# Causal mask of the row maxima: added by a TensorE matmul with the identity, the maxima by VectorE's plain negated reduction

## The reference, cut to what matters

```
q = shape_heads((hidden_states @ wq.T + bq) * scaling)
k = shape_heads(hidden_states @ wk.T + bk)
scores = jnp.einsum('bhtd,bhsd->bhts', q, k)
mask = jnp.triu(jnp.full((T, T), -10000.0, dtype=jnp.float32), k=1)
attn = jax.nn.softmax(scores.astype(jnp.float32) + mask, axis=-1).astype(jnp.float16)
out = jnp.einsum('bhts,bhsd->bhtd', attn, v)
```

## Time and profile before

| | |
|---|---|
| device time, median of 3 | 1112.86 us (1111.68 to 1113.47) |
| span of the profiled execution | 1105.8 us |
| TensorE matmul busy | 838.2 us, 76% |
| VectorE busy | 718.5 us, 65% |
| ScalarE busy | 521.4 us, 47% |
| GpSimd busy | 429.1 us, 39% |
| mean granted TensorE clock | 0.688 of full speed |

### The profile page before, as it was taken

How to read it: one execution, slowest core, us unless ns; L and a number is a source line. 1 busy time by engine, 2 the same in 40 slices (tenths; PEclk the granted TensorE clock), 3 DMA queues, 4 the chain that set the end, 5 groups by cost and what they waited for, 6 DMA issues and landing times. The chain is left out here.

```text
span 1105.8 us, 24845 instructions
## 1 busy us (share of the span) xinstructions
PE 838.2 (76%) x6684; PEld 499.3 (45%) x6685; DVE 718.5 (65%) x2639; ACT 521.4 (47%) x982; POOL 429.1 (39%) x452
## 2 busy tenths in 40 slices
PE   3698977688769678776895219999999999999600
PEld 1133433233233233332332108778778877877500
DVE  4766786787878776877875535555555555555366
ACT  2266554546446455545465015454545445454234
POOL 2145454554636546545557531222112222111224
PEclk9555555555555555555555559999999999999855
DMA  4011010210111201101110023111111111111067
GB/s 142 1 46 52 27 56 27 65 61 29 46 52 40 59 27 45 54 26 57 54 43 27 29 79 101 44 43 38 34 43 43 43 43 43 33 39 44 30 212 244
DMA packets 52749, 61.27 MB, mean 55 GB/s; under 512 B 5264, under 2 KB 39696, under 8 KB 52688
## 3 DMA queue, kind: packets, MB, share of 16 engines
q1 hardware_dynamic: 46896, 46.14, 13.9%
q0 software_dynamic: 5792, 14.49, 3.7%
HBM read 37.71 MB, written 22.90 MB: 55 GB/s over the span
## 5 line engine op out<-in xcount | busy, mean ns | idle before, releaser
L550 ACT ACTIVATE pT<-bank 128x512 f16<-128x512 f32 (+1 forms) x384 | 194.8, 527 | 241.1 <-PE bank L906 240.1
L652 DVE CUSTOM_DVE_ANT_0 unused<-bank,mask 128x384 f16<-128x384 f32 (+3 forms) x512 | 233.5, 485 | 68.3 <-PE bank L897 51.0
L897 PE MATMUL bank<-kT,qT 32*128 32x384 f16 (+3 forms) x512 | 181.3, 454 | 67.4 <-DVE nmax L652 65.1
L1354 PE MATMUL bank<-xT,gu_part 128*128 128x256 f16 (+1 forms) x1716 | 201.3, 275 | 5.0 <-issue 4.0
L1202 POOL DMA_INDIRECT expert_rows<-y_sb,dest x78 | 74.8, 959 | 315.5 <-DVE y_sb L1314 303.6
L442 POOL TENSOR_SCALAR_AFFINE_SELECT pT<-pT 128x512 f16<-128x512 f16 x128 | 80.3, 639 | 269.6 <-ACT pT L550 268.9
L1354 PEld LDWEIGHTS bank<-xT,gu_part 128*128 (+1 forms) x1716 | 166.4, 100 | 40.1 <-issue 14.0
L906 PE MATMUL bank<-qT,kT 32*128 32x384 f16 (+3 forms) x512 | 172.5, 444 | 11.5 <-ACT pT L550 11.1
L1376 PE MATMUL bank<-wd_part,h 128*128 (+1 forms) x1404 | 168.6, 273 | 1.6 <-ACT h L1235 0.2
L1376 PEld LDWEIGHTS bank<-wd_part,h 128*128 128x128 f16 (+1 forms) x1404 | 127.7, 97 | 32.8 <-issue 13.8
L1295 DVE SCALAR_TENSOR_TENSOR hid<-bank,act_g 128x512 f32<-128x512 f32 (+2 forms) x156 | 86.6, 555 | 66.8 <-ACT act_g L1228 65.6
(11 more groups left out here) (149 smaller groups left out, 1022.8 us busy)
## 6 DMA issues: line engine op xcount, KB each, us to landing
ys<-expert_rows SPq DMA_DIRECT2D x16, 512.0 KB, 4.4
st_gu<-wg SPq DMA_DIRECT2D x8, 688.0 KB, 4.1
st_gu<-wu SPq DMA_DIRECT2D x8, 688.0 KB, 4.1
st_d<-wd SPq DMA_DIRECT2D x8, 640.0 KB, 4.3
xin<-dispatch_rows SPq DMA_DIRECT2D x39, 130.0 KB, 2.3
out<-res SPq DMA_DIRECT2D x16, 256.0 KB, 2.9
x_sb<-x SPq DMA_DIRECT2D x8, 256.0 KB, 3.3
xr_sb<-x SPq DMA_DIRECT2D x8, 256.0 KB, 3.0
```

The source lines that it names most:

```text
L550: sc.activation(pT[:, lo:hi], ST_BANK[i % 2][:, 0:hi - lo], ACT.Exp, scale=1.0 / INV_SCALE).then_inc(p_ready, 1)
L652: last = v.tensor_tensor_reduce(out=unused[:, i % 2, at:at + n], in0=S_BANK[i % 2][:, at:at + n], in1=mask[:, T - n:T], scale=-1.0, scalar ...
L897: last = mm(S_BANK[i % 2][:, at:at + n], qT[32 * j:32 * j + 32, g, P * qt:P * (qt + 1)], kT[32 * j:32 * j + 32, g, 0:n], start=True, stop= ...
L1354: last = mm(dst[0:width, :], gu_part[part][:, bass.ds(col + (k * GU + at), width)], xT[j][:, k, :], start=(s == 0), stop=(s == 2 * KD - 1))
```

## The change

The mask tile becomes two 128x128 causal tiles side by side. After the scores of a step are in the bank, one more matmul adds the mask in PSUM: the identity is stationary, one mask tile is moving (two in steps 0 to 3, whose two diagonal tiles lie beside each other in columns 256 to 511). The scores' matmuls of a step so become one accumulation group with it. The maxima are plain `tensor_reduce` instructions with max and `negate=True`, with one input and no elementwise output; the tile `unused` goes.

```diff
-        mask = sb(stack, "mask", [P, T], F16)
+        mask = sb(stack, "mask", [P, 2, P], F16)
-        unused = sb(stack, "unused", [P, 2, T], F16)
...
-                ch.link(gp.memset(mask[:, :], 0.0))
-                diagonal = mask[:, T - P:T]
-                ch.link(gp.affine_select(out=diagonal, in_=diagonal, compare_op=ALU.is_ge,
-                                         fill=MASK * INV_SCALE, base=0, pattern=[[-1, P]], channel_multiplier=1))
+                ch.link(gp.memset(mask[:, :, :], 0.0))
+                ch.link(gp.affine_select(out=mask[:, :, :], in_=mask[:, :, :], compare_op=ALU.is_ge,
+                                         fill=MASK * INV_SCALE, base=0, pattern=[[0, 2], [-1, P]],
+                                         channel_multiplier=1))
...
-                        last = v.tensor_tensor_reduce(
-                            out=unused[:, i % 2, at:at + n], in0=S_BANK[i % 2][:, at:at + n], in1=mask[:, T - n:T],
-                            scale=-1.0, scalar=3.0e38, op0=ALU.add, op1=ALU.min,
-                            accum_out=nmax[:, g % 2, qt, 32 * j + HD:32 * j + HD + 1])
+                        last = v.tensor_reduce(nmax[:, g % 2, qt, 32 * j + HD:32 * j + HD + 1],
+                                               S_BANK[i % 2][:, at:at + n], AX.X, ALU.max, negate=True)
...
-                        last = mm(S_BANK[i % 2][:, at:at + n], qT[32 * j:32 * j + 32, g, P * qt:P * (qt + 1)],
-                                  kT[32 * j:32 * j + 32, g, 0:n], start=True, stop=True)
+                        mm(S_BANK[i % 2][:, at:at + n], qT[32 * j:32 * j + 32, g, P * qt:P * (qt + 1)],
+                           kT[32 * j:32 * j + 32, g, 0:n], start=(at == 0), stop=False)
                         at += n
+                    diagonal = P * tiles[0]
+                    last = mm(S_BANK[i % 2][:, diagonal:diagonal + P * len(tiles)], ident[:, :],
+                              mask[:, 0:len(tiles), :], start=False, stop=True)
                     last.then_inc(s_mm, 1)
```

## The result

The changed kernel takes 1148.72 us, the median of four runs (1146.01 to 1154.96), where the kernel before took 1112.9: a ratio of 1.033 with a 95% interval from 1.0299 to 1.0361. It is 36 us slower; forecast were 48 us, in a range that holds it. The profiled execution has a span of 1144.3 us and a time of 1146.01, so 1.7 us lie around the span. The span of 1105.8 us shown of before is that of a quick execution: in later runs on several chips the medians of before were 1107 to 1114 us.

What follows compares the result with a forecast made beforehand. TensorE's order of work at 1.2 GHz was taken to bound unhindered attention groups. Added group costs of 51.8 us, less 1 for VectorE and 3 for the clock, gave 1112.86 + 48, or 1161 us, range 1128 to 1204.

Steps and rivals of the forecast that it cites:

- an unhindered group: Attention group with no other work: TensorE's order sets its 13.55 us, and the change adds 3.5 us.
- the mask ahead of full-array work: Steps 6 to 11 of a group: the switch is paid already, so the mask costs 0.11 us a step.
- VectorE's side: Maxima: 0.015 us saved each, 0.2 us a group, as the accumulator read lies beside the next instruction; -1 us in all.
- Group 0 of a loop batch: First group in batches 2 to 6: only the last steps and the second part show, +1.0 us.
- Group 1: Second group of a loop batch: first cut 1.1 us later, GpSimd's chain of scatters not shortened, +1.2 us.
- Group 3: Fourth group of a loop batch: +1.2 us by the ranks' wait and 0.4 elsewhere, +1.6 us.
- Group 2: Third group of a loop batch: VectorE nearly full, scores 0.4 us later, then the last steps, +1.0 us in all.
- The clock: Attention stage: more full-array work gives a few more short stretches at 2.4 GHz, -3 us.
- The 7 us around the span: Time outside the profiled span, 1112.86 less 1105.8 us, taken as the same after the change.
- the clock did not hold: Rival: 2.4 GHz holds from 60 to 560 us of the attention stage, -57 us, 1056 us; chance 0.06.
- The accumulator read: Rival: dropping it gives back 1.4 us a group in about 12 groups, 1145 us; chance 0.08.
- Neither all nor nothing was hidden: Two rivals: loop waits hide all, 1131 us, chance 0.10; nothing hides, 30 groups x 3.5 + 3.0, 1221 us, chance 0.06.

Runs made afterwards that it cites:

- the mask put first: Changed kernel with the mask matmul ahead of its step's scores in steps 0 to 6: 1130.53 us, 1.0205 of the kernel before.
- 8 columns: Changed kernel with the identity matmul cut to 8 columns in place of 128 or 256: 1117.33 us, 1.0032 of the kernel before.
- own rows: Changed kernel with the mask matmul on the head's own 32 rows of the array: 1105.38 us, 0.9913 of the kernel before.
- one wait: Kernel before, with GpSimd's second scaling held from batch 1 on until VectorE's residual sum of the batch before is done: 1093.61 us, 0.9876.
- the plain reduction: Kernel before with maxima by plain negated tensor_reduce, no mask matmul, causal mask left out of the maxima: 1100.54 us, 0.9864.

## Why the prediction was right, point by point

- TensorE's order bounds an unhindered group, and its price there: right. 3.5 us forecast, 3.33 measured; steps 1.28 for 1.31 and 0.96 for 0.99, and 7.91 us for 8.08 up to L913. The two causes beside the columns were each shown: the order by the mask put first, the form by 8 columns and by own rows. Slightly too high was the mask ahead of full-array work, 0.11 for 0.08 to 0.10.
- VectorE's side: right in kind. The read lay beside the next instruction, and a maximum gained 0.01, not 0.09. By the reading of the Trainium skill's "VectorE: DVE Perf Modes", "The DRAIN you can't avoid", the read would have been worth its full length; it was not in any kernel here. The same section says that an operation that is not held starts earlier, which the prediction left out and which is what these rows show.
- Group 0 of a loop batch: +1.0 forecast, +0.5 measured. Group 1: +1.2 and +1.9. Its first cut came 1.06 us later, as thought (1.1), but the chain from the first cut to the last, forecast to stay at 12.03, took 12.90. Group 3: +1.6 and +2.0.
- Group 2: wrong, and the largest miss. Forecast +1.0, measured -1.3. The step that failed is "VectorE is nearly full": I took 17.24 of 18.22 us busy for work. Of this, 2.5 us a batch was a sum waiting for GpSimd inside its own busy time, and the change moved GpSimd out of its way. The 3.2 us wait for maxima in the earlier trace rows was its mark, and I asked only whether the new matmuls would fit below it, not what made it long.
- The clock: right in kind (eight short stretches in the attention stage behind its start, three before), too small. I took -3 us. Against groups of the same place at 1.2 GHz, the stretches saved about 11 us in the first trace of the changed kernel (of 1.2, 2.5, 0.4, 2.6, 2.5 and 2.2 us) and 1.5 in that of before. One such stretch saves 2.5 us in the changed kernel where TensorE sets the pace, and 0.7 before.
- The sum of 48 us came as near to the measured 36 as it did partly by luck: 12 too much in group 2 over five batches, 7 too little of clock, and a few single microseconds the other way. The moved meeting, of which the prediction knew nothing, was most of the difference: against the two kernels that lost the meeting by one wait or by the plain reduction, the changed one is slower by about 50 us. The 7 us around the span were wrong too (1.7 measured), without effect on the difference.
- The rivals: the clock did not hold (0.50 with TensorE busy 16.88 of 16.88 us; the rule of "TensorE: Matmul & The Clock Gate" in the Trainium skill, section "Why this matters for your kernels", that a TensorE kept busy gets the full clock, is contradicted by that group). The accumulator read did not count. Neither all nor nothing was hidden: of the 3.3 us, a loop group kept 0.8 on average.

## What to carry to other kernels

A busy engine may be waiting: take one instruction's minimum and maximum duration over its executions before calling it work, and look at what the other engine runs beside the long ones. When 32-row and 128-row matmuls share TensorE, count the two switches and the neighbours that can no longer run side by side: up to L913 of an unhindered group they cost more than the columns, in the whole kernel about half as much. Put the full-array work where a switch is paid already. When a change of order wins or loses a few per cent, test for a moved collision by removing it from both kernels, as it hid about a quarter of the price here.

## What the runs showed of the hardware

- VectorE's f16 residual sum (0.68 us alone) that starts 0.05 us or more behind a GpSimd tensor_tensor ends 0.55 us after that has ended: 2.75 us of scaling made it 3.23 or 2.57 by how early it met it. Where it started ahead, or at most 0.03 us behind, it kept its 0.68 and the scaling took 3.20 to 3.32. A sum of 32 elements from f32 to f16 went from 0.18 to 2.05 us beside GpSimd's subtraction of 2.60 us, and ended 0.05 us behind it. The maxima from PSUM beside the same scaling kept their durations. By the Trainium skill ("SBUF — State Buffer", "Who interferes with whom") a VectorE instruction with two inputs in SBUF contends with a GpSimd instruction that reads SBUF; these rows agree, and in the prediction I did not weigh it.
- Changing TensorE from 32 to 128 rows took 0.13 us at 1.2 GHz and changing back 0.11, with 8, 128 or 256 columns in between.
- The granted clock rose for short stretches of the attention stage. In the two traces of the changed kernel each began in or just behind the projections and value matmuls at the end of a group; before, one of three began just behind L913 of group 1, which follows the output projection. The kernel with fewer full-array columns (eight a mask) had more of them than the changed one, so I can't say what decides. The profile's clock can also be wrong: in the 8-column kernel's trace it reads 1.00 from 24 to 83 us, where 512 columns take 0.60 us as they do at 0.50 until 80.
